# Second expert layer in pairs and single units of 128 slots, with results stored per token and summed at the end

## The chip, the cores and the metric

The kernel runs on one core of a Trainium2 chip, in float32 with float16 pairs (a high and a low part) for the second expert layer. The metric is the device time of one execution in microseconds, the median of the runs shown.

## The reference

The program is two transformer-like layers over x of 4 x 256 tokens (1024 in all) and 256 channels. Each layer is attention on a conditioned x, then a mixture of experts on a conditioned x, both added to x. The change lies in the last step, the experts of the second layer:

```python
gate_weights = softmax(x @ Wg + bg)                      # 8 experts
topv, topi = top_k(gate_weights, 2)
h  = gelu(x @ W1[n] + b1[n])                              # 256 -> 512
h  = gelu(h @ W2[n] + b2[n])                              # 512 -> 512
eo = h @ W3[n] + b3[n]                                    # 512 -> 256
out = sum over n of eo[n] * comb[:, n]                    # comb: topv at topi, else 0
x = x + out
```

## The kernel before

All stages before are left as they are: the conditioning, the first layer's attention, its experts in 47 tiles of 128 slots, the second layer's attention. While the second layer's attention runs, the expert weights are split into float16 pairs and stored in DRAM (`split1`, 2 MB for each expert), and the tokens are routed in three parts (the first four blocks of 128 tokens, then two, then two): `choose1`, `sum_tiles`, `combine`, `place_rows` on VectorE, `ranks1` and `turn_combination` on TensorE. A token's row (high and low parts of 256 channels, its eight combination weights, its number) is scattered by GpSimd to the DRAM array `slots` (L521), once for each of its two experts, each expert having a region of 1024 rows. 16 such indirect DMAs are issued.

Then come 15 tiles (TILES) of 256 slots (SLOTS), enough for any split of 2048 rows over 8 experts. VectorE works out a table (the expert and the first row of each tile), and SP reads it for the addresses of its loads. For tile j:

- SP loads the rows (`tile_rows`, four buffers; from tile 4 on after `added`, that is when the stores of tile j-4 have landed) and the 2 MB of weights with the biases (`tile_weights`, three buffers; when the third layer of tile j-3 is done). All loads have the line of the helper `load`, L323.
- TensorE turns the rows (`turn_tile`, L2247), then `first`, `second`, `third`: 24, 48 and 24 matmuls (three products for each pair of high and low parts; all in the helper at L1668), weights stationary and 256 slots moving in the first two, and slots stationary, 256 channels moving in the third. The order is written out: second(j), turn_tile(j+2), first(j+1), third(j).
- ScalarE copies the turned rows (`tile_out`, L836), applies Gelu for each of four chunks of a layer (`hidden`, L844), and scales the results by the combination weight (`rows_weighed`, L853, into two buffers).
- VectorE picks the weights (`pick`, L1645 and L1647) and splits the hidden values into high and low (`split_hidden`, L1652 and L1654).
- GpSimd adds the results to `out` by an indirect DMA with an addition at the destination (L532). Two tiles may hold the same token, so each tile's stores wait until the earlier tile's have landed.

`out` holds the base rows beforehand: x plus the biases b3 weighed by the combination (`base_rows`, `base_bias` on TensorE, banks 2 to 5; the copy at L831 on ScalarE), which SP stores as one DMA of 1 MB (L450) before the first accumulating store. Tile 0's turn on TensorE waits until all four parts of the base are copied.

## Time and profile before

| | us |
|---|---|
| median of 3 runs | 1161.17 |
| lowest, highest | 1158.29, 1168.63 |
| profiled execution: span, first to last instruction | 1139.7 |
| what lies around the span, against the median | 21.5 |

The page gives the span of one profiled execution and no other time for it; the median of the runs is 21.5 us longer. Of this span TensorE is busy 85%, VectorE 71%, ScalarE 51%, GpSimd 19%. PE is a TensorE matmul, PEld its load of stationary weights, DVE VectorE, ACT ScalarE, POOL GpSimd, SP SyncE, which issues the plain DMAs. The tiles of the second expert layer fill the time from about 944 us to the end.

### The profile page before, as it was taken

To read this page: it belongs to the slowest core of one execution; us is meant where nothing else is said; L and a number is where in the kernel's file an instruction comes from. 1 tells how busy PE (TensorE), PEld (TensorE's weight loads), DVE (VectorE), ACT (ScalarE), POOL (GpSimd) and SP (SyncE) were. 2 spreads that over 40 slices of the span, in tenths; PEclk is the share of its full clock that TensorE was granted. 3 is DMA by queue.
4 is the path that set the end of the run, shared out by engine and by line. 5 is a ranking of instruction groups with operands and counts; after the bars stand their busy time and mean duration, and the time that the engine had idled before them with its cause. 6 is when DMAs were issued, how large, how long until landed. Compare 5 with 4: busy or idle time off the path is not lost.

```text
span 1139.7 us, 18485 instructions
## 1 busy us (share of the span) xinstructions
PE 972.8 (85%) x6328; PEld 699.0 (61%) x6328; DVE 809.2 (71%) x2082; ACT 580.9 (51%) x1444; POOL 211.1 (19%) x175
## 2 busy tenths in 40 slices
PE   3898989997998799789987889689889976998995
PEld 2677767776777677553655566423333365987884
DVE  7689888888888879983487885766666763554542
ACT  2398439844884488441232332147566723544542
POOL 1101110111011101047233333100000050323223
PEclk9999999999999989989999999979999978999998
DMA  9999700000000000034588885325455547777762
GB/s 264 241 233 231 180 1 1 2 1 1 1 1 1 1 2 1 1 137 169 178 273 269 268 279 168 136 98 199 163 205 207 189 145 279 231 224 206 245 202 28
DMA packets 75966, 161.31 MB, mean 142 GB/s; under 512 B 10706, under 2 KB 57310, under 8 KB 71776
## 3 DMA queue, kind: packets, MB, share of 16 engines
q1 hardware_dynamic: 66992, 145.52, 41.9%
q0 software_dynamic: 8880, 14.60, 5.0%
q8 instruction: 51, 0.84, 0.3%
q14 instruction: 43, 0.35, 0.1%
HBM read 127.68 MB, written 62.62 MB: 167 GB/s over the span
## 4 chain that ended last, share of the span: by engine, by line
PE 46%; DVE 19%; DMA 17%; ACT 7%; issue 5%; POOL 3%; SPq 2%; POOLq 0%; ACTq 0%; DVEq 0%
PE ps L1668 43%; DMA out<-arena 8%; DMA arena<-in_w0all 4%; DMA made<-arena 3%; DVE arena L1449 2%; POOL out L532 2%; DVE arena L1108 2%; DVE arena L1125 1%; DMA arena<-slots 1%; ACT arena L632 1%; DVE arena L1117 1%; POOL slots L521 1%; ACT arena L617 1%; DVE arena L1141 1%; DVE arena L1079 1%
## 5 line engine op out<-in xcount | busy, mean ns | idle before, releaser
L1668 PE MATMUL ps<-arena 128*128 128x256 f16 (+14 forms) x4712 | 764.7, 338 | 57.0 <-DMA arena<-in_w0all 18.4
L1668 PEld LDWEIGHTS ps<-arena 128*128 128x128 f32 (+8 forms) x4712 | 529.0, 148 | 224.6 <-issue 94.8
L1652 DVE CAST arena<-arena 128x256 f16<-128x256 f32 x120 | 37.4, 311 | 96.4 <-ACT arena L844 96.4
L1449 DVE TENSOR_REDUCE arena<-ps 128x4 f16<-128x1024 f32 (+1 forms) x48 | 58.8, 1228 | 50.5 <-PE ps L1668 50.4
L844 ACT ACTIVATE arena<-ps,arena 128x256 f32<-128x256 f32 x120 | 55.6, 473 | 57.9 <-PE ps L1668 57.7
L1141 DVE SCALAR_TENSOR_TENSOR arena<-arena 128x128 f32<-128x128 f32 x240 | 84.0, 412 | 0.5
L469 POOL TENSOR_TENSOR den<-den,backd 128x512 f32<-128x512 f32 x8 | 10.5, 1307 | 393.4 <-DVE euv L946 393.4
L632 ACT ACTIVATE arena<-ident,arena 128x128 f32<-128x128 f32 x256 | 81.0, 391 | 0.0
L532 POOL DMA_INDIRECT out<-arena x30 | 47.5, 1584 | 146.6 <-DMA out<-arena 84.5
L501 POOL DMA_INDIRECT made<-arena x47 | 53.0, 1128 | 105.9 <-DVE arena L1362 105.4
L751 ACT ACTIVATE arena<-ps 128x1024 f32<-128x1024 f32 x48 | 49.2, 1024 | 43.4 <-PE ps L1668 43.4
L1108 DVE SCALAR_TENSOR_TENSOR arena<-arena,ps 128x128 f32<-128x128 f32 (+1 forms) x128 | 47.2, 410 | 26.9 <-PE ps L1668 20.4
L965 DVE RECIPROCAL den<-den 128x128 f32<-128x128 f32 x64 | 56.6, 923 | 0.4
L1654 DVE TENSOR_TENSOR arena<-arena 128x256 f16<-128x256 f32 x120 | 51.1, 426 | 4.1
L521 POOL DMA_INDIRECT slots<-side x16 | 15.6, 973 | 204.8 <-DVE side L1535 200.2
L617 ACT ACTIVATE arena<-arena 128x128 f32<-128x128 f32 (+1 forms) x128 | 50.3, 440 | 0.0
L719 ACT ACTIVATE arena<-ps 128x176 f32<-128x176 f32 x47 | 14.9, 318 | 65.4 <-PE ps L1668 65.4
L1668 PE MATMUL ps<-causal,identb 128*128 128x256 bf16 x160 | 36.4, 311 | 12.9 <-DVE arena L1449 10.1
L610 ACT ACTIVATE arena<-arena 128x128 f32<-128x128 f32 (+1 forms) x128 | 47.3, 441 | 0.0
L1125 DVE TENSOR_TENSOR arena<-ident,arena 128x512 f32<-128x512 f32 x64 | 46.2, 727 | 0.1
L1117 DVE CUSTOM_DVE_ANT_0 arena<-arena 128x128 f32<-128x128 f32 (+1 forms) x128 | 46.3, 399 | 0.0
L1479 DVE TENSOR_TENSOR arena<-arena 128x512 f16<-128x512 f32 x64 | 42.4, 684 | 4.9 <-ACT arena L791 4.9
(283 smaller groups left out, 1255.2 us busy)
## 6 DMA issues: line engine op xcount, KB each, us to landing
arena<-split SPq DMA_DIRECT2D x14, 2048.0 KB, 9.2
arena<-in_w0all SPq DMA_DIRECT2D x47, 608.0 KB, 5.1
slots<-in_blank SPq DMA_DIRECT2D x17, 1040.0 KB, 16.5
arena<-in_w1all SPq DMA_DIRECT2D x16, 1024.0 KB, 6.6
split<-arena SPq DMA_DIRECT2D x32, 512.0 KB, 3.8
slots<-in_blank SPq DMA_DIRECT2D x9, 1072.0 KB, 18.7
arena<-slots SPq DMA_DIRECT2D x47, 130.0 KB, 3.4
side<-made SPq DMA_DIRECT2D x8, 512.0 KB, 5.2
```

Of the source, the lines that this page charges most:

```text
L501: pool.indirect_dma_start(made0[:], bass.IndirectOffsetOnAxis(ap=ids, axis=0), y0[:, j % Y0N], None, bounds_check=K0 * NT - 1, oob_is_err= ...
L532: pool.indirect_dma_start(out[:], bass.IndirectOffsetOnAxis(ap=ids, axis=0), ytok[:, j % 2, half], None, compute_op=ALU.add).then_inc(adde ...
L617: ins = act.activation(prob[:, n % 3, cols], prob[:, n % 3, cols], ACT.Copy, scale=rinv[:, n % 2, tt:tt + 1])
L632: ins = act.activation(diag_post[:, n % 4, 2 * tt + i], ident[:], ACT.Copy, scale=mixw[:, tt, 3, i, n:n + 1])
L844: act.activation(hfull[:, m], ps[:, m, 0:SLOTS], ACT.Gelu, bias=bias[:, j % 3, 4 * layer + m:4 * layer + m + 1]).then_inc(l_read, 1)
L965: st(dve.reciprocal(part, part))
L1108: ins = dve.scalar_tensor_tensor(logit[:, s, tiles[tt]], rankq[:, 0, tiles[tt]], mixw[:, tt, 0, 2, n:n + 1], ps[:, s, tiles[tt]], ALU.mult ...
L1117: ins = dve.tensor_tensor_reduce(logit[:, s, tiles[tt]], logit[:, s, tiles[tt]], second[:, s, tiles[tt]], -1.0, 3.0e38, ALU.add, ALU.min, ...
L1125: dve.tensor_tensor(diag_pre[:, n % 4].rearrange("p (t i) j -> p t i j", t=TT), spread(spread(ident[:], 1, 2), 1, TT), spread(mixw[:, :, 1 ...
L1141: ins = dve.scalar_tensor_tensor(dst, prob[:, n % 3, tiles[tt]], w, dst, ALU.mult, ALU.add)
L1449: dve.tensor_reduce(out, ps[:, at:at + 2].rearrange("p j (r s) -> p j r s", r=nr), X, ALU.max, negate=True).then_inc(max1_done, 1)
L1668: return pe.matmul(o, l, r, start=start, stop=stop, skip_group_check=shared)
```

## The change

The tiles become 23 units of 128 slots, in 16 tiles: 7 pairs (256 slots) and 9 singles (128 slots), in the fixed order pair, single, pair, single, pair, single, single, and so on. Each tile still loads its expert's 2 MB once. The table gives each expert's pairs first and its left-over unit as a single. The first two layers move 128 columns for a single; the third has one half.

The eight combination weights in a row are replaced by five numbers (first weight, twice the token's number, difference of the second weight to the first, one, and the second expert). `pick` works out a slot's weight and its destination: 2 x token + choice. Results go by plain indirect stores, up to eight tiles deep in `ytok`, to a DRAM array `made1` with a row for each token and choice. At the end SP loads `made1` in four parts of 512 KB, VectorE adds the two choices and the base rows, and SP stores `out` in four parts of 256 KB. The base rows stay in SBUF, tokens laid out eight to a partition, so `base_rows` and `base_bias` take columns with a step of 8. The first base rows now wait for all of x, and all four `base_bias` for the last combination. The store of base rows to `out` and the wait for it are gone. The rows of tiles 0, 1 and 2 are requested before the rest of tile 0's weights and before tile 1's; the second layer's weights of tile 0 are requested with the first layer's.

```diff
 TILES0 = (NT * K0 + E0 * (P - 1)) // P
 W0WORDS = 2 * 2 * I0 + 2 * C
 SHUNITS = 2 * (-(-SH0 // P))
-TILES = (NT * 2 + E1 * (SLOTS - 1)) // SLOTS
-ROW = C + E1 + 4
+UNITS = (NT * 2 + E1 * (P - 1)) // P
+PAIRS = (UNITS - E1) // 2
+SINGLES = UNITS - 2 * PAIRS
+TILES = PAIRS + SINGLES
+SIZES = [2, 1] * 2 + [2, 1, 1] + [2, 1] * 2 + [2, 1, 1] + [2, 1]
+assert SIZES.count(2) == PAIRS and SIZES.count(1) == SINGLES
+UNIT0 = [sum(SIZES[:j]) for j in range(TILES + 1)]
+TABLE_AT = [SIZES[:j].count(2) if n == 2 else PAIRS + SIZES[:j].count(1) for j, n in enumerate(SIZES)]
+SLOTS = 2 * P
+MADE = Y0N
+ROW = C + 5
...
+        def stored1(j):
+
+            first_layer = (TILES0 + MADE - 1 - j % MADE) // MADE
+            return 16 * (first_layer + sum(SIZES[i] for i in range(j % MADE, j + 1, MADE)))
 
...
 
             def tile_rows(j):
-                row = sp.value_load(table[0:1, 16 + j:17 + j], min_val=0, max_val=E1 * REGION + 3 * SLOTS)
+                t, n = TABLE_AT[j], SIZES[j]
+                row = sp.value_load(table[0:1, 16 + t:17 + t], min_val=0, max_val=(E1 + 2) * REGION - SLOTS)
                 if j >= 4:
-                    sp.wait_ge(added, 32 * (j - 3))
-                load(rows_in[:, j % 4], slots[bass.ds(row, SLOTS)].rearrange("(a p) c -> p a c", p=P), x_in1[j % 4])
+                    sp.wait_ge(XT_pe, j - 3)
+                    sp.wait_ge(w_picked, j - 3)
+                load(rows_in[:, j % 4, 0:n], slots[bass.ds(row, n * P)].rearrange("(a p) c -> p a c", p=P), x_in1[j % 4])
...
             sp.wait_ge(scattered, 16 * 2 * TAU)
-            tile_rows(0)
-            tile_rows(1)
+            for j in range(3):
+                tile_rows(j)
             tile_weights(0, 1)
-            tile_weights(1)
-            sp.wait_ge(base_ready, 4)
-            sp.dma_start(out[0:NT].rearrange("(a p) c -> p a c", p=P), base).then_inc(base_out, 16)
             for j in range(1, TILES):
-                if j > 1:
-                    tile_weights(j)
-                if j + 1 < TILES:
-                    tile_rows(j + 1)
+                tile_weights(j)
+                if j + 2 < TILES:
+                    tile_rows(j + 2)
+            for n in range(MADE):
+                sp.wait_ge(made_out[n], stored1(TILES - MADE + n))
+            both = made1[0:2 * NT].rearrange("(p a k) c -> p a k c", a=TAU, k=2)
+            for q in range(TAU // 2):
+                load(planes[:, 2 * q:2 * q + 2], both[:, 2 * q:2 * q + 2], x_in1[q])
+            rows = out.rearrange("(p a) c -> p a c", a=TAU)
+            for q in range(TAU // 2):
+                sp.wait_ge(out_summed, q + 1)
+                sp.dma_start(rows[:, 2 * q:2 * q + 2], base[:, 2 * q:2 * q + 2]).then_inc(out_stored, 16)
+            sp.wait_ge(out_stored, 16 * (TAU // 2))
 
...
             for j in range(TILES):
-                pool.wait_ge(x_in1[j % 4], 16 * (j // 4 + 1))
-                if j:
-                    pool.wait_ge(added, 32 * j)
-                for half in range(2):
-                    pool.wait_ge(y1_read, 2 * j + half + 1)
-                    ids = rows_in[:, j % 4, half, C + E1:C + E1 + 1].bitcast(U32)
-                    pool.indirect_dma_start(out[:], bass.IndirectOffsetOnAxis(ap=ids, axis=0), ytok[:, j % 2, half], None,
-                                            compute_op=ALU.add).then_inc(added, 16)
-            pool.wait_ge(added, 32 * TILES)
+                pool.wait_ge(w_picked, j + 1)
+                for half in range(SIZES[j]):
+                    pool.wait_ge(y1_read, UNIT0[j] + half + 1)
+                    ids = idslot[:, 2 * (j % 4) + half:2 * (j % 4) + half + 1]
+                    pool.indirect_dma_start(made1[:], bass.IndirectOffsetOnAxis(ap=ids, axis=0), ytok[:, j % MADE, half], None,
+                                            bounds_check=2 * NT - 1, oob_is_err=False).then_inc(made_out[j % MADE], 16)
+            for n in range(MADE):
+                pool.wait_ge(made_out[n], stored1(TILES - MADE + n))
...
                 st.settle()
-                st.tell(dve.tensor_tensor(rows_out[:, part, C:C + E1], placed[:, 0, part], placed[:, 1, part], ALU.add),
+                st(dve.tensor_copy(rows_out[:, part, C], top1[:, part, 0]))
+                st(dve.tensor_tensor(rows_out[:, part, C + 2], top1[:, part, 1], top1[:, part, 0], ALU.subtract))
+                st(dve.tensor_copy(rows_out[:, part, C + 4], idf1[:, part, 1]))
+                st.tell(dve.tensor_tensor(comb1[:, part], placed[:, 0, part], placed[:, 1, part], ALU.add),
                         comb_ready, told)
...
             def pick(j):
+                n, t, rows = SIZES[j], TABLE_AT[j], rows_in[:, j % 4]
                 dve.wait_ge(x_in1[j % 4], 16 * (j // 4 + 1))
-                st(dve.tensor_tensor(picked, rows_in[:, j % 4, :, C:C + E1], spread(mine[:, j], 1, 2), ALU.mult))
-                st.settle()
-                st.tell(dve.tensor_reduce(wslot[:, j % 4], picked, X, ALU.add), w_picked, j + 1)
-
-            def split_hidden(dst, c):
+                if j >= 4:
+                    dve.wait_ge(y1_read, UNIT0[j - 3])
+                    dve.wait_ge(made_out[j % MADE], stored1(j - MADE))
+                st(dve.scalar_tensor_tensor(picked[:, 0:n], spread(rows[:, 0:n, C + 4], 2, 2), tile_e[:, t:t + 1],
+                                            rows[:, 0:n, C + 2:C + 4], ALU.is_equal, ALU.mult))
+                st.settle()
+                st(dve.tensor_tensor(wslot[:, j % 4, 0:n], picked[:, 0:n, 0], rows[:, 0:n, C], ALU.add))
+                st.tell(dve.tensor_tensor(idslot[:, 2 * (j % 4):2 * (j % 4) + n], picked[:, 0:n, 1], rows[:, 0:n, C + 1],
+                                          ALU.add), w_picked, j + 1)
...
             for j in range(TILES):
                 pick(j)
-                split_hidden(h2, 4 + 8 * j)
+                split_hidden(h2, j, 4 + 8 * j)
                 if j + 1 < TILES:
-                    split_hidden(h1, 8 + 8 * j)
+                    split_hidden(h1, j + 1, 8 + 8 * j)
+            for q in range(TAU // 2):
+                both, here = planes[:, 2 * q:2 * q + 2], base[:, 2 * q:2 * q + 2]
+                dve.wait_ge(x_in1[q], 16 * (TILES // 4 + 1))
+                st(dve.tensor_tensor(both[:, :, 0], both[:, :, 0], both[:, :, 1], ALU.add))
+                st.settle()
+                st.tell(dve.tensor_tensor(here, here, both[:, :, 0], ALU.add), out_summed, q + 1)
...
             def base_rows(q):
                 for half in range(2):
-                    tok = slice((2 * q + half) * P, (2 * q + half + 1) * P)
+                    tok = slice(2 * q + half, NT, TAU)
                     for k in range(CT):
...
             project_out(B - 1)
-            base_rows(0)
-            base_rows(1)
             ranks1(slice(HEAD, HEAD + TT), 2)
             route(wg1, E1, 5, range(HEAD + TT, TAU))
             turn_rows(3)
-            pe.wait_ge(combT_ready, 1)
-            base_bias(0)
-            base_bias(1)
+            pe.wait_ge(x_done, 2 * B)
+            base_rows(0)
+            base_rows(1)
             pe.wait_ge(low_ready, 3)
             base_rows(2)
             ranks1(slice(HEAD + TT, TAU), 3)
@@ -2231,8 +2286,8 @@
             pe.wait_ge(low_ready, 4)
             base_rows(3)
             pe.wait_ge(combT_ready, 2)
-            base_bias(2)
-            base_bias(3)
+            for q in range(TAU // 2):
+                base_bias(q)
 
...
             def layer(j, n, src, nk, c):
+                slots_in = slice(0, SIZES[j] * P)
                 for m in range(4):
                     if c + m >= 4:
                         pe.wait_ge(l_read, c + m - 3)
                     for k in range(nk):
                         for a, b in ((0, 0), (0, 1), (1, 0)):
-                            ins = mm(ps[:, m, 0:SLOTS], weights(j, a, n, k, slice(m * P, (m + 1) * P)), src[:, b, k],
+                            ins = mm(ps[:, m, slots_in], weights(j, a, n, k, slice(m * P, (m + 1) * P)), src[:, b, k, slots_in],
...
@@ -2280,12 +2336,13 @@
                 pe.wait_ge(h_split, 8 * j + 8)
                 if j == 0:
                     pe.wait_ge(w_in1[0], 32)
-                for half in range(2):
-                    if j:
-                        pe.wait_ge(y1_read, 2 * (j - 1) + half + 1)
+                for half in range(SIZES[j]):
+                    u = UNIT0[j] + half
+                    if u >= 2:
+                        pe.wait_ge(y1_read, u - 1)
                     for k in range(4):
                         for a, b in ((0, 0), (0, 1), (1, 0)):
-                            ins = mm(ps[:, 4 + half, 0:C], h2[:, b, k, half * P:(half + 1) * P],
+                            ins = mm(ps[:, 4 + u % 2, 0:C], h2[:, b, k, half * P:(half + 1) * P],
                                      weights(j, a, 2, k, slice(0, C)), k + a + b == 0, k == 3 and a == 1)
```

## Rows read from the trace of the kernel before

**Rows 1.** The page, TensorE's granted clock in 40 slices, in tenths of full speed.

```profile
PEclk9999999999999989989999999979999978999998
```

**Rows 2.** The chain that ended last, in order of time: start us, us, what.

```profile
979.76 1.56 POOL out L532
...
981.63 8.75 DMA out<-arena
```

**Rows 3.** Timeline of TensorE, tiles: start us, us, instructions [idle before <-releaser].

```profile
953.21 5.41 PE L1668 MATMUL ps<-arena 128*128 128x256 f16 x48 [1.80 <-DVE arena L1654]
...
962.13 0.62 PE L2247 MATMUL ps<-ident,arena 128*128 128x128 f16 x8 [3.50 <-DMA arena<-slots]
962.58 10.64 PE L1668 MATMUL ps<-arena 128*128 128x256 f16 x96
973.06 0.61 PE L2247 MATMUL ps<-ident,arena 128*128 128x128 f16 x8
...
1101.35 0.62 PE L2247 MATMUL ps<-ident,arena 128*128 128x128 f16 x8 [0.66 <-DMA arena<-slots]
...
1124.28 2.79 PE L1668 MATMUL ps<-arena 128*128 128x256 f16 x24 [1.35 <-DVE arena L1654]
```

**Rows 4.** Windows: busy us of each engine, TensorE's clock, DMA share, GB/s.

```profile
936.00:962.00 26.00, 14.15 (x94) 10.77 (x93) 5.74 (x18) 8.20 (x13) 0.47 (x1) 0.73 0.84 287
...
1038.00:1050.00 12.00, 11.42 (x109) 10.03 (x108) 6.03 (x19) 5.75 (x12) 3.29 (x2) 1.00 0.75 221
...
1110.00:1122.00 12.00, 12.00 (x112) 10.77 (x110) 6.92 (x20) 5.42 (x12) 6.31 (x4) 1.00 0.29 33
```

**Rows 5.** DMA issues: KB each, median us to landing; last, the one load at 956.44.

```profile
arena<-split SPq DMA_DIRECT2D x14, 2048.0 KB, 9.2
...
split<-arena SPq DMA_DIRECT2D x32, 512.0 KB, 3.8
...
made<-arena POOLq DMA_INDIRECT x47, 4.9
...
DMA to landing us min/median/max: 10.6/10.6/10.6
```

**Rows 6.** Groups by shape, TensorE's loads of weights: count, busy us, mean ns.

```profile
L1668 PEld LDWEIGHTS ps<-arena 128*128 128x128 f16 x1440 | 141.1, 98 | 20.4 <-DVE arena L1654 3.7
```

**Rows 7.** Timeline of SP's queue, start of the tiles and one later tile.

```profile
948.09 0.51 SPq L450 DMA_DIRECT2D out<-arena  x1
...
992.22 0.33 SPq L323 DMA_DIRECT2D arena<-split  x1
```

**Rows 8.** Groups by shape, VectorE, nearest to a single's split.

```profile
L1425 DVE CAST arena<-arena 128x128 f16<-128x128 f32 x4 | 0.9, 227 | 0.1
L1432 DVE TENSOR_TENSOR arena<-arena 128x128 f16<-128x128 f32 x4 | 1.2, 292 | 0.1
```

**Rows 9.** Timeline, the base rows and the start of tile 0.

```profile
934.77 3.77 PE L1668 MATMUL ps<-arena 8*128 8x256 f32 x8 [2.61 <-DVE arena L1539]
...
944.01 1.01 PE L2247 MATMUL ps<-ident,arena 128*128 128x128 f16 x8 [5.47 <-DMA arena<-slots]
...
947.04 4.38 PE L1668 MATMUL ps<-arena 128*128 128x256 f16 x24
```

**Rows 10.** Timeline, the end of the first layer's tiles, and the last tile.

```profile
701.64 0.98 POOL L501 DMA_INDIRECT made<-arena  x1 [1.18 <-DVE arena L1362]
703.89 10.24 SPq L323 DMA_DIRECT2D side<-made  x8
...
707.67 0.69 DVE L1381 TENSOR_TENSOR side<-side 128x512 f32<-128x512 f32 x1 [6.80 <-DMA side<-made]
709.10 0.69 DVE L1381 TENSOR_TENSOR side<-side 128x512 f32<-128x512 f32 x1 [0.73 <-DMA side<-made]
...
1125.89 0.47 ACT L853 ACTIVATE arena<-ps,arena 128x256 f32<-128x256 f32 x1 [2.44 <-PE ps L1668]
1127.15 1.55 POOL L532 DMA_INDIRECT out<-arena  x1 [5.27 <-ACT arena L853]
```

175 lines of the change are left out of this document (100 added, 75 removed).

## The prediction, on record before the result

> **What bounds the kernel now.** I read the page's first two parts: TensorE is busy 85%, its granted clock is full but for a few slices [rows 1]. That is an average; the change touches only the last fifth of the span, so I went on to the chain that ended last [rows 2]. From 979.76 us on it alternates between GpSimd's issue of an accumulating store (1.56 us) and its landing (8.75 us and more), and the next tile's first store waits for that landing: with two issues a tile this comes round every 11.4 us or later. This is one limit.
>
> The second limit is TensorE itself [rows 3]. One tile's turn starts at 962.13, the next at 973.06: a period of 10.93 us in which TensorE does not stop: 8 turns of 128 columns in 0.45 us (56 ns each, each with its own load of weights), then 96 matmuls of 256 columns from 962.58 to 973.06, 109.2 ns each. From 962.13 to 1101.35 there are 12 periods, 139.22 us; 12 x 10.93 is 131.16, so the chain of stores adds only 8.1 us, visible as waits for the rows of a later tile (0.66 us at 1101.35). The idle TensorE that the chain can be charged with is small, since both limits are about equal: removing the chain alone is worth little, and shortening TensorE alone would leave the chain.
>
> The third candidate is the DMA. In 1038 to 1050 it is 0.75 busy at 222 GB/s [rows 4]. In 1110 to 1122, where no more weights come, three accumulating stores (131 KB each) take 0.29 of 12 us, 1.16 us apiece. Taking two of them out of a tile's 9.0 us leaves 6.7 us for 2.37 MB, 354 GB/s; in 936 to 962, with few of them, it is 287 GB/s at 0.84, or 342 GB/s. A 2 MB load needs the engines 6.2 us then, but its landing takes 9.2 us in the median [rows 5].
>
> **The change part by part.** *Tiles.* Before: 15 tiles of 256 slots, 30 units of 128. After: 7 pairs and 9 singles, 23 units in 16 tiles. A pair costs the old 10.93 us. A single has 72 matmuls of 128 columns, 12 of 256 and 4 turns. The trace has no matmul of 128 columns on these weights; the nearest are the turns, f16, 128 x 128, with a load each: 56 ns. So 72 x 0.056 + 12 x 0.109 + 0.22 = 5.5 us. Stage: 7 x 10.93 + 9 x 5.5 = 126.3 against 15 x 10.93 = 163.95: **-37.6 us**. The upper end for the 128-column matmul is the mean duration of one load, 98 ns [rows 6]; I take 56 because the turns have a load of the same size each and still follow each other every 56 ns, so a load's duration overlaps its neighbours.
>
> The Trainium skill, TensorE: Matmul & The Clock Gate, Back-to-back issue gap, gives about 81 ns sustained for a stream of load and 128-column matmul, and its section LDWEIGHTS gives P/1.2, which for 128 columns is an estimate of 107 ns. By the first the 648 matmuls would cost 16 us more than by the row, by the second 33 us more. The turns' 56 ns in this trace disagree with both.
>
> *Waits that go.* With plain stores in eight buffers nobody waits for a landing: the 8.1 us above go. At the start, TensorE ends the second layer of tile 0 at about 958.6 and waits 3.5 us for tile 2's rows [rows 3], which lie behind the 1 MB store of the base rows in the queue [rows 7]; the store goes and the rows are asked for before the weights. The last tile's 1.35 us before its third layer goes with the old kernel too: **-12.9 us** together.
>
> *Waits that come.* (a) Weights. They have three buffers: the load of tile j leaves when the third layer of j-3 is done. SP needs some 0.9 us more, an estimate (it issues the biases, then the weights, 0.33 us of issue each [rows 7]), then 9.2 to land: 10.1. Where j-2 and j-1 are a pair and a single, TensorE has second 5.25 or 2.7, first 1.34 or 2.62, third 2.62 or 1.31, second 2.7 or 5.25, and turns, some 12.5 us: covered. Where both are singles (twice), it has 2.69 + 1.34 + 1.31 + 2.69 + 0.67 = 8.7: 1.4 us late, 2.8 in all. (b) Splitting. ScalarE's Gelu and VectorE's split stand between a layer's last group and the next layer. For 256 columns this takes 1.35 us (the wait at 1124.28 [rows 3]); the cover is the third layer of the tile before, 2.62 behind a pair but 1.31 behind a single. VectorE's 0.67 us a chunk keeps pace with 0.66 of TensorE for a pair; for a single, 0.23 + 0.29 [rows 8] beside matmuls of 0.34 a chunk lags slightly. I allow 2 us (0 to 6), and 1.3 at the last tile, where no first layer covers. Together **+6.1 us**, between 1.3 and 11. ScalarE takes 0.47 us a chunk of 256 [rows 10] and less for 128, eight and some copies in a single's 5.5 us: under the bound. GpSimd's issues, 23 of about 1.1 us, are hidden, as are the two or three small VectorE steps that choose weight and address of a row.
>
> *The head.* Three small VectorE steps are added to each of three parts of the routing; the last two lie ahead of a wait of VectorE for TensorE's ranks, of about the same length. On TensorE the base rows of tiles 0 to 3 move behind the turn of the last rows, in the place of four of the base's bias products (some 1.9 us, half of the eight at 934.77 [rows 9]): 16 matmuls of 128 float32 columns, an estimate of 1.8 to 3.7 us from those, by the clock. All four bias products now come after the last combination: eight took 3.8 us at 934.77, so 16 take 7.5, after a table of tiles that is some five VectorE steps (1 us) longer. Tile 0's turn waits for that: 936 + 7.5 and the copy give 944.5, against 943.98 before [rows 9]; GpSimd's 16 scatters, which end at their own pace, and the load of tile 0's rows give about the same. Behind them are the first three loads of rows and the first weights. A TensorE that has not stopped for 5 us may get its full clock back earlier than before, where the first layer took 4.38 us for 24 matmuls at half clock: -1.8. The base rows' strided weights may cost a little. **+0.5 us** (-2 to +4).
>
> *The tail.* Before: last matmul 1126.9 (1124.28 and 24 x 0.109), end 1139.7, 12.8 us. After: last matmul, copy 0.5, GpSimd 0.8 later (1126.36 to 1127.15 [rows 10]), store landed and seen 2.25 us after (701.64 to 703.89, the same drain in the first layer [rows 10]), or 4.9 where the DMA is busy [rows 5]. Then four loads of 512 KB: the first is usable 3.8 us after issue, the next 1.43 us later [rows 10], so the last at 8.1; two additions of 0.69; 0.5 to SP; a store of 256 KB, 3.4 us, from 512 KB at 3.8. Sum 0.5 + 0.8 + 2.25 + 8.1 + 1.5 + 0.5 + 3.4 = 17.05: **+4.3 us** (+2 to +8).
>
> Sum: -37.6 - 12.9 + 6.1 + 0.5 + 4.3 = -39.6 us. The profiled execution has a span of 1139.7; the median of the runs shown is 21.5 above it, which I leave as it is. 1161.2 - 39.6 = 1121.6, say **1121.5 us**, 3.4% faster.
>
> **Rivals.** *The load of weights sets the pace.* There are 16 loads of 2 MB instead of 15, in less time. If a load can't overlap the one before, 13 loads (tiles 3 to 15) at 9.2 us run from 10 us after the start of tile 0's second layer to 129.8; the last third layer is done 9 us later, 10 us after my 129 for this stretch. At the 10.6 us that a load took beside other traffic (the last of [rows 5]) it is 28 us. That gives 1131 to 1150. For it: 38 MB in 128 us is near 300 GB/s. Against: the 342 to 354 GB/s above, and the accumulating stores go, 35 us of engine time. *The narrow matmul is paced by its load*: 648 x (98 - 56) ns = 27 us, 1149. Against it are the turns' 56 ns. The Trainium skill's two figures above would put it at 1137 and 1155. *The clock falls.* The granted clock was 0.73 in 936 to 962, where TensorE was busy 14.15 of 26 us, and 1.00 through all of the later waits for rows [rows 4]. If waits for weights were dense enough to hold it at half (1.2 GHz), each microsecond of work costs another; the 39.6 us are gone once a third of the 123 us of work run at half, and with all of it the time is some 1240. That is the way to slower; nothing in the stretches at full clock supports it.
>
> **How the numbers follow.** Forecast 0.66, loads pace 0.19, narrow matmuls 0.09, clock 0.04, and 0.02 that the reordered head stalls more than I see (the change's stage then gives back less). The forecast's own bounds: added waits down to 1.3, head -2 and tail +2 give 1112; 11, +4 and +8 give 1134. The range reaches to 1110 for the scatter of the runs and to 1140 for half of the loads' rival, and leaves out the upper half of it and the 98 ns case. About 1% (1149.6 us and 1172.8 us) is what a measurement of this kernel can tell from no change, its runs lie 10 us apart. Faster by over 1%: 0.66 and most of 0.19 and of the 98 ns case: 0.91. Within 1%: 0.05; slower: 0.04.
>
> **What would show it.** The accumulating stores' waits are gone from the chain, TensorE dominates it up to the last 17 us. Matmuls of 128 columns start 56 ns apart; from tile 0's second layer to the last third layer 129 us. Weight waits appear before tiles 7 and 14, of 1 to 3 us; if they stand before every tile, it is the loads' rival, with the DMA share over 0.9. The granted clock is 1.00 throughout. Tile 0 is turned at 944 to 946. The prediction is wrong if singles take clearly more than 5.5 us, if 2 MB loads land in over 11 us while others are under way, or if the drain at the end is over 20 us.

## The result, and the profile after

The changed kernel takes 1128.38 us in the median of its runs (1115.46 to 1130.91), the kernel before 1161.17 us (1155.19 to 1168.63): a ratio of 0.970, 95% interval 0.965 to 0.976. That is 3.0% faster by the ratio, and 32.8 us less by the medians; 1121.5 us was forecast, with a range of 1110 to 1140. A ratio counts only executions within 1.5% of the fastest of their kernel; on chip A below, that leaves four of the thirteen of the kernel before, so the ratios there are cautious and their intervals wide.

The profiled execution has a span of 1113.6 us and took 1115.46 us, so only 1.9 us lie around the span. The profile of before has 1139.7 us, 21.5 below its median; if as little lies around that span, the gap is inside it. It was then an execution of some 1141.6 us, 13.6 below the fastest of its five runs. Its chip is not on record. So I compare stretches of the traces, not whole spans. Four stretches give the whole difference of the spans: up to the first turned combination 923.47 against 916.69 (+6.8, in code that the change hardly touches); from there to tile 0's second layer 41.87 against 36.52 (+5.3); from there to the last matmul 132.3 against 173.7 (-41.4); from there to the end 15.95 against 12.8 (+3.2). The sum is -26.1, as 1113.6 - 1139.7.

The windows of the changed kernel: the tiles, twelve microseconds out of them, and the end (busy us of PE, PEld, DVE, ACT, POOL, then the granted clock, DMA share, GB/s).

```profile
965.00:1098.00 133.00, 125.98 (x1484) 113.91 (x1484) 76.06 (x297) 65.04 (x161) 21.79 (x22) 1.00 0.69 249
1040.00:1052.00 12.00, 11.35 (x131) 10.24 (x129) 6.45 (x25) 5.68 (x13) 1.92 (x2) 1.00 0.67 256
1098.00:1113.00 15.00, 0.00 (x0) 0.00 (x0) 5.35 (x8) 0.42 (x1) 0.98 (x1) 0.58 0.59 210
```

TensorE works 95% of the tiles' stretch, at full clock throughout. The DMA is busy 0.69 of it, and in the twelve microseconds 0.67, less than the 0.75 of before [rows 4] with 35 GB/s more moved. The timeline of TensorE (start, us, instructions, [idle before <- what ended it]):

```profile
965.34 5.41 PE L1725 MATMUL ps<-arena 128*128 128x256 f16 x48 [1.35 <-DVE arena L1704]
970.59 0.61 PE L2302 MATMUL ps<-ident,arena 128*128 128x128 f16 x8
971.04 6.80 PE L1725 MATMUL ps<-arena 128*128 128x128 f16 x96
977.68 0.39 PE L2302 MATMUL ps<-ident,arena 128*128 128x128 f16 x4
977.90 4.09 PE L1725 MATMUL ps<-arena 128*128 128x256 f16 x36
982.56 5.41 PE L1725 MATMUL ps<-arena 128*128 128x256 f16 x48 [0.56 <-DVE arena L1704]
...
1016.60 2.85 PE L1725 MATMUL ps<-arena 128*128 128x128 f16 x48 [0.66 <-DVE arena L1704]
1019.29 0.39 PE L2302 MATMUL ps<-ident,arena 128*128 128x128 f16 x4
1019.51 9.63 PE L1725 MATMUL ps<-arena 128*128 128x256 f16 x84
...
1096.34 1.48 PE L1725 MATMUL ps<-arena 128*128 128x256 f16 x12 [1.83 <-DVE arena L1704]
```

Read the group of 96 at 971.04: tile 1's first layer (24 of 128 columns), tile 0's third (24 of 256), tile 1's second (48 of 128). It runs to the turn at 977.68, 6.64 us; with 24 x 0.1092 for the wide ones, a narrow one takes 56 ns. The only things that end an idle time of TensorE in this stretch are VectorE's splits (L1704), 7.6 us in ten rows with the 1.35 at its start. No row waits for weights: the first layer of tile 7 starts at 1019.51, right behind the turn.

The end, from all engines' timeline:

```profile
1099.25 0.98 POOL L555 DMA_INDIRECT made<-arena  x1 [5.03 <-ACT arena L880]
1101.45 1.76 SPq L340 DMA_DIRECT2D fac<-made  x4
1105.37 0.69 DVE L1716 TENSOR_TENSOR fac<-fac 128x512 f32<-128x512 f32 x1 [9.09 <-DMA fac<-made]
1106.82 4.50 SPq L481 DMA_DIRECT2D out<-arena  x4
1110.27 0.69 DVE L1718 TENSOR_TENSOR arena<-arena,fac 128x512 f32<-128x512 f32 x1
```

From the last matmul (1097.65) to the last store's issue 1.6 us, 2.2 until its landing is seen, 3.9 to the first addition, 5.6 over the four parts, 2.6 for the last store.

### The profile page after: what moved, and what is told of

Read it like the earlier page. It is cut to its first block, busy times and chain, and to the rows that moved or that the text cites. A ratio compares the mean times of both kernels' runs of the same rounds, so it can differ in the third digit from the quotient of the medians.

```text
span 1113.6 us, 18547 instructions
## 1 busy us (share of the span) xinstructions
PE 946.8 (85%) x6288; PEld 676.7 (61%) x6288; DVE 804.9 (72%) x2140; ACT 566.4 (51%) x1446; POOL 186.1 (17%) x168
## 4 chain that ended last, share of the span: by engine, by line
PE 54%; DVE 22%; DMA 9%; ACT 8%; issue 5%; SPq 1%; another core or an unknown queue 0%; POOL 0%; ACTq 0%; POOLq 0%; DVEq 0%
PE ps L1725 50%; DMA made<-arena 4%; DMA arena<-in_w0all 3%; DVE arena L1475 2%; DVE arena L1134 2%; DVE arena L1704 2%; DVE arena L1151 1%; ACT arena L656 1%; DVE arena L1143 1%; ACT arena L641 1%; DVE arena L1167 1%; DVE den L991 1%; DVE arena L1105 1%; ACT arena L634 1%; DVE arena L1702 1%
## 5 line engine op out<-in xcount | busy, mean ns | idle before, releaser
L1725 PE MATMUL ps<-arena 128*128 128x128 f32 (+15 forms) x4700 | 739.3, 333 | 64.6 <-DMA arena<-in_w0all 17.2
L1725 PEld LDWEIGHTS ps<-arena 128*128 128x128 f32 (+8 forms) x4700 | 505.6, 149 | 228.8 <-issue 99.6
L1702 DVE CAST arena<-arena 128x128 f16<-128x128 f32 (+1 forms) x128 | 32.8, 256 | 67.1 <-ACT arena L870 57.2
L870 ACT ACTIVATE arena<-ps,arena 128x128 f32<-128x128 f32 (+1 forms) x128 | 48.1, 418 | 49.1 <-PE ps L1725 44.4
L528 POOL DMA_INDIRECT made<-arena x47 | 53.0, 1127 | 107.8 <-DVE arena L1388 106.4
L1134 DVE SCALAR_TENSOR_TENSOR arena<-arena,ps 128x128 f32<-128x128 f32 (+1 forms) x128 | 47.2, 410 | 26.9 <-PE ps L1725 20.4
L548 POOL DMA_INDIRECT slots<-side x16 | 15.6, 972 | 208.2 <-DVE side L1564 203.9
L1704 DVE TENSOR_TENSOR arena<-arena 128x128 f16<-128x128 f32 (+1 forms) x128 | 45.3, 354 | 4.4
L1725 PE MATMUL ps<-causal,identb 128*128 128x256 bf16 x160 | 36.4, 311 | 12.8 <-DVE arena L1475 10.1
L1505 DVE TENSOR_TENSOR arena<-arena 128x512 f16<-128x512 f32 x64 | 42.5, 684 | 4.7 <-ACT arena L815 4.5
L555 POOL DMA_INDIRECT made<-arena x23 | 22.8, 990 | 130.8 <-DVE arena L1695 110.6
```

Of the source, the lines that this page charges most:

```text
L528: pool.indirect_dma_start(made0[:], bass.IndirectOffsetOnAxis(ap=ids, axis=0), y0[:, j % Y0N], None, bounds_check=K0 * NT - 1, oob_is_err= ...
L1134: ins = dve.scalar_tensor_tensor(logit[:, s, tiles[tt]], rankq[:, 0, tiles[tt]], mixw[:, tt, 0, 2, n:n + 1], ps[:, s, tiles[tt]], ALU.mult ...
L1704: st.tell(dve.tensor_tensor(dst[:, 1, m, 0:n], hfull[:, m, 0:n], dst[:, 0, m, 0:n], ALU.subtract), h_split, c + m + 1)
L1725: return pe.matmul(o, l, r, start=start, stop=stop, skip_group_check=shared)
```

## The experiments

Every ratio is to the kernel before, run on the same chip. The kernels ran in three groups, each on one chip: A (the first four below), B (the next four), C (the last four). The stretches are those of above, "head" from the first turned combination to tile 0's second layer, all in us.

| kernel | chip | median | ratio, interval | head | tiles | end |
|---|---|---|---|---|---|---|
| before, changed | - | 1161.2, 1128.4 | 0.970 (0.965 to 0.976) | 36.5, 41.9 | 173.7, 132.3 | 12.8, 15.9 |
| changed_again | A | 1125.8 | 0.974 (0.961 to 0.986) | 41.9 | 132.2 | 16.3 |
| pairs_only | A | 1157.3 | 1.001 (0.994 to 1.009) | 42.5 | 161.9 | 16.1 |
| rows_first | A | 1123.6 | 0.972 (0.963 to 0.982) | 39.1 | 132.4 | 15.9 |
| base_late | A | 1122.8 | 0.970 (0.955 to 0.984) | 42.2 | 132.4 | 15.8 |
| adding_chain | B | 1108.3 | 0.965 (0.962 to 0.969) | 40.1 | 130.3 | 16.7 |
| singles_last | B | 1109.8 | 0.966 (0.963 to 0.970) | 40.3 | 132.6 | 16.1 |
| pad_dve | B | 1105.8 | 0.964 (0.959 to 0.968) | 39.8 | 128.6 | 15.9 |
| rows_turns | B | 1104.5 | 0.962 (0.959 to 0.965) | 37.8 | 127.3 | 15.8 |
| changed_third | C | 1121.5 | 0.969 (0.962 to 0.975) | 41.9 | 132.2 | 16.0 |
| pairs_adding | C | 1158.0 | 0.995 (0.990 to 0.999) | 42.1 | 161.9 | 16.9 |
| rows_turns_again | C | 1126.1 | 0.969 (0.965 to 0.974) | 39.1 | 131.4 | 15.9 |
| three_edits | C | 1121.5 | 0.966 (0.960 to 0.971) | 38.7 | 131.5 | 15.9 |

The chip of the first row is not on record. The three medians of the changed kernel lie 0.6% apart, the executions of one kernel on one chip up to 2.3% (before, on A); head and tiles of the changed kernel's traces on A and C agree within 0.1 us, the end within 0.4. Where an edit is worth under 5 us, its verdict therefore rests on the stretches.

**changed_again** and **changed_third** are the changed kernel itself.

> The changed kernel once more, on the chip that also runs the three variants below, so that their traces have a neighbour. Expected: a time of 1115 to 1131 us; from the start of tile 0's second layer to the last third layer 132 us, as in its first trace. If the 6.8 us by which everything before the tiles was later in that trace belongs to the change, it is there again; if it is the scatter of single executions, it is another number.

> The changed kernel again, as the base for the other three kernels of this call. From the ratios to the kernel before that it had so far (0.970 and 0.974) it should come out 2.6 to 3.3% below it. If VectorE's hole of 3.3 us ahead of the last logits belongs to the program, it is here too; the four runs without it so far were all variants on another chip than the rest, so if it belongs to the chip, this run has it or not with all three others.

Both repeat the gain, with intervals clear of 1, and both have the hole of VectorE: an idle time of 3.3 us ahead of the last logits, for which the trace shows no releaser in the program (its rows stand at base_late).

**pairs_only.** All tiles are pairs again (15 of 256 slots), with everything else of the change kept.

```diff
-PAIRS = (UNITS - E1) // 2
-SINGLES = UNITS - 2 * PAIRS
+PAIRS = (NT * 2 + E1 * (2 * P - 1)) // (2 * P)
+SINGLES = 0
...
-SIZES = [2, 1] * 2 + [2, 1, 1] + [2, 1] * 2 + [2, 1, 1] + [2, 1]
+SIZES = [2] * PAIRS
```

> The new way of storing and summing, with the old tiles: 15 pairs, no singles. If the narrow tiles carry the gain (my account), this gives nearly all of it back: 15 tiles of 10.93 us, 161 us from tile 0's second layer to the last third layer against 132, and a time near 1157 us, 0 to 1% under the kernel before. If the chain of adding stores was what bound the old kernel, freeing it is most of the gain: about 1135 us.

The whole gain is gone, while the tiles still are 11.8 us shorter than before (161.9 against 173.7). So the narrow units are worth 161.9 - 132.2 = 29.7 us. Of the 11.8 us by which the tiles are shorter otherwise, 9.3 are paid out again at both ends: +6.0 and +3.3.

**adding_chain.** The units kept, the stores to `made1` made adding ones, each tile's only after the landing of the tile's before (`made1` is filled with zeros early on).

```diff
                 pool.wait_ge(w_picked, j + 1)
+                if j:
+                    pool.wait_ge(made_out[(j - 1) % MADE], stored1(j - 1))
...
-                                            bounds_check=2 * NT - 1, oob_is_err=False).then_inc(made_out[j % MADE], 16)
+                                            bounds_check=2 * NT - 1, oob_is_err=False,
+                                            compute_op=ALU.add).then_inc(made_out[j % MADE], 16)
```

> The units are kept (7 pairs, 9 singles), but the results go by stores that add at the destination, as before the change, each tile's only after the earlier tile's have landed. My reading of the profile of before: an issue takes about 1.56 us (the first of a pair is joined by the second) and a landing 8.75 us, so the chain comes round every 11.4 us for a pair and about 10 us for a single. 16 tiles then last 7 x 11.4 + 9 x 10 = 170 us against the 132 us of the changed kernel: about 1128 + 38 = 1165 us, the whole gain gone, with TensorE idle behind it through the eight buffers only at the end. Rival (an adding store lands faster when there is less to move, so TensorE stays the bound): the stage stays within 5 us of 132, 1128 to 1135 us.

My expectation fell, the rival holds: 0.965, tiles of 130.3. That is 1.7 us above the 128.6 of pad_dve, the changed kernel but for the pad, on the same chip, and it is no cost of the chain: tile 0's second layer, before the first store, takes that much longer. The granted clock was 0.50 in its first 3.4 us, and 1.00 throughout in pad_dve. The same 48 matmuls in adding_chain, then in pad_dve:

```profile
961.19 7.07 PE L1730 MATMUL ps<-arena 128*128 128x256 f16 x48 [2.03 <-DVE arena L1709]
```

```profile
959.15 5.41 PE L1729 MATMUL ps<-arena 128*128 128x256 f16 x48 [1.72 <-DVE arena L1708]
```

GpSimd's timeline of adding_chain:

```profile
972.78 1.61 POOL L559 DMA_INDIRECT made<-arena  x1 [30.22 <-DVE arena L1700]
974.69 1.58 POOL L559 DMA_INDIRECT made<-arena  x1 [0.30 <-issue]
983.63 1.56 POOL L559 DMA_INDIRECT made<-arena  x1 [7.35 <-DMA made<-arena]
990.40 1.55 POOL L559 DMA_INDIRECT made<-arena  x1 [5.22 <-ACT arena L885]
```

A pair's round, from its first issue to the next tile's, is 10.9 us here, but a single's only 6.8 and then ended by ScalarE, not by the landing. Over all tiles a single's round takes 5.2 to 7.4 us, and the landing ends about half of them: one adding store needs less time to land than two behind each other. I had taken "about 10 us" for a single from a pair's row and only dropped one issue.

**pairs_adding.** The edits of pairs_only and adding_chain together.

> Both parts undone in the tiles: 15 pairs and the adding stores with the wait for the earlier tile's, on top of the new end. Alone, pairs cost the whole gain (ratio 1.0013), and the adding chain with units cost nothing (0.9653). Theory: the chain of adding stores is as long as TensorE's work in either kernel, 11.2 to 11.4 us for a pair and 6 to 7 for a single, so it costs little beside a pair too: tiles of 162 us (as with plain stores) plus up to 8 us, ratio 1.00 to 1.01. Rival: the chain alone was worth the 10 us by which the old stage (173.7) exceeds the new one with pairs (161.9): ratio 1.010 to 1.015.

The tiles are 161.9 us with adding stores as with plain ones. So the plain stores are worth nothing in them, with wide tiles either. TensorE stands still for no landing in this kernel. The DMA queues of the kernel before (965 to 1125), then of this one (985 to 1140), each with 28 stores: packets, MB, share of 16 engines; the last figure of the x28 row is the median us to landing.

```profile
q0 software_dynamic: 4032, 3.67, 16.0%
...
out<-arena POOLq DMA_INDIRECT x28, 9.4
```

```profile
q0 software_dynamic: 4032, 2.11, 9.4%
```

28 stores of 131 KB are 3.67 MB; 2048 rows of 1 KB are 2.1 MB. With the check of bounds, which the change adds to the store, the rows of empty slots (3840 slots for 2048 rows) move nothing.

In the kernel before, nine stalls of TensorE at its turns are for rows, 10.2 us together. The first, 3.5 us [rows 3], is for tile 2's rows, which lay behind the 1 MB store of the base rows in the queue; that store is gone in this kernel too. The other eight are for rows of a tile j that were asked for only once tile j-4's stores had landed. Now the rows wait only until the buffer has been turned and picked from, empty rows move nothing, and results have eight buffers instead of two. These carry the other 8 us. Which of them carries how much was not tried.

**rows_first.** The rows of tiles 0 to 2 are asked for ahead of the 1 MB of tile 0's second layer's weights, as before the change. The first layer's weights stay ahead of the rows.

```diff
-                        load(wtile[:, 0, :, one:two], parts[:, :, one:two], ld["shared"])
                         return
+                    load(wtile[:, 0, :, one:two], parts[:, :, one:two], ld["shared"])
```

> The 1 MB of tile 0's second-layer weights is requested after the rows of tiles 0 to 2, as before the change. If the rows wait in the DMA behind these weights (6.7 us from request to landing in the changed kernel, 2.9 before), tile 0's turn comes 3 to 4 us earlier after the request; tile 0's second layer follows 2 to 4 us earlier unless its weights are then late. If the rows were slow for another reason, nothing moves. The time: 2 to 4 us less, less than the scatter, so the trace decides.

The stretch to tile 0's second layer is 2.7 us shorter than in the changed kernel beside it. The change had asked for the second layer's weights of tile 0 early, and its rows wait behind them in the queue: they landed 6.7 us after their request, against 2.9 before. Not all of that comes back, since another limit is close behind: tile 0's turn now waits 0.69 us for ScalarE's copy of the base rows.

**base_late.** The base rows of tiles 0 to 3 go behind the second turned combination.

```diff
-            pe.wait_ge(x_done, 2 * B)
-            base_rows(0)
-            base_rows(1)
             pe.wait_ge(low_ready, 3)
...
             turn_combination(1)
+            pe.wait_ge(x_done, 2 * B)
+            base_rows(0)
+            base_rows(1)
             pe.wait_ge(low_ready, 4)
```

> The base rows of tiles 0 to 3 are computed after the last ranks and the last combination's turn instead of ahead of them. If these 16 float32 matmuls at the half clock hold back the ranks and so the last four scatters (3 us in the changed kernel's trace), GpSimd's wait of 3.7 us before its last four scatters goes and they end some 3 us earlier; the base itself is complete no earlier and may then bound tile 0's turn. Rival: the ranks wait for VectorE anyway and nothing moves.

Nothing moved: TensorE then waited 5.5 us for VectorE, which makes the input of the ranks. The cause stands in the trace of the changed kernel, VectorE's timeline: it sits idle ahead of the last logits (L1511), although the routing products had ended about 931.7.

```profile
931.12 0.17 DVE L1564 CAST side<-side 128x4 uint32<-128x4 f32 x1
934.58 0.17 DVE L1511 TENSOR_TENSOR side<-ps,arena 128x16 f32<-128x16 f32 x1 [3.29 <-remote]
```

**pad_dve.** 64 writes to unused columns, before the first layer's tiles, move VectorE's stream of instructions.

```diff
+            for n in range(64):
+                st(dve.memset(small[:, 48 + n % 16:49 + n % 16], 0.0))
+                if n % 16 == 15:
+                    st.settle()
             middle(0)
```

> 64 one-column writes into unused columns are put into VectorE's instruction stream before the first layer's tiles; they cost under 5 us where they stand (64 x about 0.06 us, and VectorE is not the bound there), and nothing else is changed. In every trace of the changed kernel VectorE stands still for 3.3 us with no visible releaser before the last part of the logits (line 1511), and the kernel before has no such hole. If the hole comes from the position of the instruction in the stream (its index is 2046, 2 short of 8 x 256), the pad moves it away: the ranks, the last scatters and the turn of tile 0 come up to 3 us earlier counted from the first turned combination, total 1125 to 1129. If it comes from something that VectorE really waits for, the hole stays where it is and the total is 1128 to 1133.

The hole is gone, but in all four traces of chip B, the three without the pad too. The timeline of singles_last on B, the same two instructions and then TensorE:

```profile
926.67 0.17 DVE L1564 CAST side<-side 128x4 uint32<-128x4 f32 x1
...
927.28 0.17 DVE L1511 TENSOR_TENSOR side<-ps,arena 128x16 f32<-128x16 f32 x1 [0.44 <-PE ps L1725]
...
927.99 5.82 PE L1725 MATMUL ps<-ident,xT 128*128 128x128 f32 x24
...
933.64 0.73 PE L1725 MATMUL ps<-side,before_after 128*128 128x16 f32 x6
934.23 0.60 PE L2252 MATMUL ps<-ident,side 128*8 128x128 f32 x4
934.41 0.17 DVE L1555 TENSOR_TENSOR side<-ps,arena 128x16 f32<-128x16 f32 x1 [2.25 <-PE ps L1725]
```

So the pad tells nothing of its own, and the position in the stream is refuted as the sole reason: the same instructions have the hole on A and C and not on B. Nor does it always stand there: in pairs_adding, on C, VectorE waits only 0.45 us before the last logits, but 1.23, 1.16 and 1.46 us at later instructions. singles_last does show what stands behind the hole: the 24 float32 products of the base rows (5.82 us) hold the ranks, and VectorE waits 2.25 us for them, where it waited 1.05 in the kernel before.

**singles_last.** `SIZES` is seven pairs, then nine singles.

> Same work, other order: seven pairs, then nine singles in a row. It asks what the alternation of pair and single is worth. A single is 6.2 to 7 us of TensorE, and every one needs 2 MB. Theory (loads overlap, the DMA engines need about 6.5 us for 2 MB, a load lands some 9 to 10 us after its request, three buffers): a little below the DMA's capacity, waits for weights of 0 to 1.4 us a single, 0 to 12 us in all, plus 0.7 us for each single behind a single in place of one behind a pair: 1128 to 1142 us, with DMA shares near 0.95 in the singles. Rival (a load cannot overlap the one before, 9.2 us apiece): 8 x (9.2 - 6.5) = 22 us and more, 1150 us or over. If neither wait shows, 1125 to 1131.

The singles' windows and two of their rows on TensorE:

```profile
1040.00:1050.00 10.00, 9.37 (x139) 8.42 (x137) 6.78 (x32) 5.52 (x15) 1.74 (x2) 1.00 1.04 423
1050.00:1060.00 10.00, 8.80 (x139) 8.17 (x136) 6.78 (x29) 6.05 (x17) 1.21 (x2) 1.00 0.93 326
```

```profile
1041.77 2.85 PE L1725 MATMUL ps<-arena 128*128 128x128 f16 x48 [0.31 <-DVE arena L1704]
...
1047.98 2.85 PE L1725 MATMUL ps<-arena 128*128 128x128 f16 x48 [0.17 <-DVE arena L1704]
...
1052.09 2.83 PE L1725 MATMUL ps<-arena 128*128 128x128 f16 x36 [1.02 <-DMA arena<-split]
```

A single comes round in 6.0 to 7.1 us, with 2 MB each at a DMA share about 1. The loads overlap, and the waits for weights (1.02, 0.44, 1.13) sum to 2.6 us, the low end of the 0 to 12 expected. The tiles take 4.0 us more than in pad_dve, but 1.7 of that is the granted clock in tile 0's second layer (48 matmuls in 7.08 us), as in adding_chain. The rival, a load that can't overlap the one before, is refuted; so is a large worth of the alternating order.

**rows_turns**, run on two chips. rows_first, and where tile j is a single, the turn of tile j+2 behind the first layer of tile j+1 (on ScalarE its copy likewise).

```diff
-                if j + 2 < TILES:
+                if j + 2 < TILES and SIZES[j] == 2:
                     turn_tile(j + 2)
                 if j + 1 < TILES:
                     first(j + 1)
+                if j + 2 < TILES and SIZES[j] == 1:
+                    turn_tile(j + 2)
                 third(j)
```

> Two edits together: the rows of tiles 0 to 2 are requested before the first 1 MB of weights (measured alone: tile 0's second layer starts 2.7 us earlier), and where tile j is a single, the turn of tile j+2 is put behind the first layer of tile j+1 instead of ahead of it, so that it covers the split before the next second layer. In the changed kernel seven such places wait 0.56 to 0.67 us for VectorE; the turn is 0.22 to 0.45 us. Theory: each shrinks by that, at the cost of the same cover before the third layer of the single, which had 0.3 us to spare: between 0 and 3 us less. 1128 - 2.7 - 1.5 = 1124 us. Rival (ScalarE's copy of the turned rows now stands ahead of the scaling of results, or the split before the third layer becomes late): no gain from the second edit or up to 3 us of loss, 1125 to 1129.

> The two edits of before, rows first and the turn behind the first layer where the tile is a single, now beside the changed kernel on one chip. In its trace the split waits in the tiles fell (2.97 us of waits in all against 6 to 7 in the changed kernel's, but on another chip). Theory: 2.7 us from the rows and 1 to 4 us from the turns, 4 to 6.5 us less than the changed kernel beside it. Rival: the fewer split waits belong to the chip, and only the rows' 2.7 us are left.

The rows' edit repeats (head -2.8 us on C; -1.9 on B, against pad_dve). The turns shorten the tiles by 1.3 us on B (127.3 against 128.6 in pad_dve) and 0.8 on C (131.4 against 132.2): the low end of what I expected. The tiles, now reached earlier, wait for weights instead: 1.9 us in two rows on B, 0.5 in one on C. In the medians nothing of it shows: 0.969 on both sides on C, with the median of this kernel 4.6 us above that of the changed one. On C seven waits for splits are left in the tiles (4.4 us), on B one (1.05): the fewer waits belong to the chip, as the rival had it.

**three_edits** adds base_late to them.

> The same two edits, and the base rows of tiles 0 to 3 behind the ranks and the second turned combination. That edit alone moved nothing (base_late) where VectorE had its hole of 3.3 us. Where the hole is absent, the ranks' input is ready at 930.85 us (line 1527) and TensorE takes it at 933.64, after 24 float32 matmuls of the base rows that stand in front. Theory: without the hole, the last scatters, and with them tile 0, come 2 to 2.8 us earlier than in the kernel with two edits, if TensorE gets the base rows done in the wait for the scatters' landing, 5 us long; with the hole 0. Rival: the base rows then end behind the landing of tile 0's rows and hold the turn of tile 0: 0 to 3 us slower.

On C, with the hole, the head gets 0.4 us shorter: TensorE does the base rows in its wait for the scatters, up to the biases' products, and the turn waits 1.3 us for rows (0.7 for ScalarE's copy of the base without the edit). Three edits together make the smallest ratio on C (0.966 against 0.969), but the intervals overlap widely; in the stretches it is 4.0 us better than the changed kernel. The case that I meant, this kernel without the hole, was not measured, since this kernel ran on a chip with it.

## Why the prediction was right, and where it was not

**Sum.** By stretches I had forecast +0.5 for the head, -44.4 for the tiles (-37.6 - 12.9 + 6.1) and +4.3 for the end. The trace gives +5.3, -41.4 and +3.2. The differences, +4.8, +3.0 and -1.1, are 6.7 us; the median is 6.9 above the forecast. That the two agree so closely is luck: the three stretches leave out the 6.8 us ahead of the head, and the traces are single executions. Nor are the two traces alike. That of before has none of the pauses told of below, like those on chip B; the first of the changed kernel has them, like those on A and C. Like against like, with pad_dve, the stretches give +3.3, -45.1 and +3.1, together -38.7 us against the forecast -39.6, and each of the three within 3 us.

**Tiles, narrow units: right.** 56 ns for a 128-column matmul with a load of its own, taken from the turns, is what was measured. The load's 98 ns [rows 6] are how long one load lasts and not the pace, so that rival is out. Net of the waits that narrow units bring, I had them at 37.6 - 6.1 = 31.5 us; pairs_only gives 29.7. On chip B the padded kernel, otherwise the changed one, has tiles of 128.6 us where I forecast 129.

**Waits that go: right sum, and a wrong reason for most of it.** My 12.9 us were 8.1 for the landing of the accumulating stores, 3.5 for rows behind the store of the base, and 1.35 at the last tile. pairs_only, without narrow units, has tiles 11.8 us shorter than before, where the first two make 11.6. The last tile's wait did not go: 1.36 us there, and 1.83 in the changed kernel. For the 3.5 the reason fits: the store is gone, the rows are asked for earlier, and the wait is gone. The step "With plain stores in eight buffers nobody waits for a landing: the 8.1 us above go" named the wrong part. pairs_adding has the adding stores and GpSimd's wait for landings, and its tiles are as short. By elimination, what held TensorE was the rows of a later tile, asked for behind `added`, together with landings that were slow while empty rows moved too; no run undid one of these alone. The check of bounds on the new store stood in the diff, and I did not price it.

**Waits for weights: covered by another wait.** 2.8 us were forecast before tiles 7 and 14; none came in the first trace. The need was about right: the third layer of tile 4 ends at 1009.4, the load of tile 7 goes out at 1010.24, and the first layer of tile 7 starts 10.1 us after the former. But my 8.7 us for the work between was short of the split waits that stand in it (0.27 and 0.66 in the rows, and smaller gaps). The two terms are not additive. On B, where one of those waits is absent, 0.27 us for weights shows before tile 7.

**Splits: too small.** 2 + 1.3 us forecast, 6.2 measured behind the start (ten rows with 7.6 in all, less 1.35), plus smaller gaps. The 6.2 hold the last tile's 1.83, forecast at 1.3. Six of the waits stand before a second layer behind a single, 0.56 to 0.67 us each in the first trace, and are there on A and C too. The two before the second layer of a single stand in pad_dve on B as well (0.70 us each); the four before a pair's don't, and the last tile waits 1.05 there instead of 1.83. What B lacks comes with a pause of ScalarE in the second layer of the single in front. The changed kernel, then the padded one on B:

```profile
975.87 0.37 ACT L870 ACTIVATE arena<-ps,arena 128x128 f32<-128x128 f32 x1 [0.20 <-PE ps L1725]
...
976.58 1.11 POOL L555 DMA_INDIRECT made<-arena  x1 [0.30 <-issue]
977.41 0.37 ACT L870 ACTIVATE arena<-ps,arena 128x128 f32<-128x128 f32 x1 [1.17 <-PE ps L1725]
```

```profile
969.68 0.37 ACT L870 ACTIVATE arena<-ps,arena 128x128 f32<-128x128 f32 x1 [0.19 <-PE ps L1729]
...
970.35 0.37 ACT L870 ACTIVATE arena<-ps,arena 128x128 f32<-128x128 f32 x1 [0.30 <-PE ps L1729]
970.38 1.11 POOL L555 DMA_INDIRECT made<-arena  x1 [0.30 <-issue]
```

Two chunks of Gelu start 0.67 us apart on B and 1.54 on the other chip, and TensorE goes on alike at this place: from the first of these two to the next turn it is 1.81 us in both. The pause stands beside GpSimd's second issue in these rows. So it does in all seven tiles with a second issue, with ScalarE idle for 1.1 to 1.9 us; in pad_dve, on B, in none of the seven. That the issue causes it was not tried. The tiles are 3.7 us longer with the pauses than in pad_dve.

**Head: +5.3, not +0.5.** This step failed, beyond its bound of +4; on B, without the holes, the head is +3.3 to +3.8, just inside it. The premise that failed is "GpSimd's 16 scatters, which end at their own pace". Before, they did. In the changed kernel GpSimd waits for the last ranks before its last four scatters. The last scatter in the kernel before, then the first of the last four in the changed one:

```profile
935.51 0.96 POOL L521 DMA_INDIRECT slots<-side  x1 [0.30 <-issue]
```

```profile
941.91 0.96 POOL L548 DMA_INDIRECT slots<-side  x1 [3.73 <-DVE side L1564]
```

The wait is 3.5 to 3.8 us in all traces of A and C, and 2.0 on B. Counted from the first turned combination the last scatter ends 3.4 us later than before (pad_dve: 1.7), from there to tile 0's turn it takes 1.9 us more (2.0), and from the turn to the second layer as long as before, 9.2 us (8.8 on pad_dve). These are the 5.3 us.

Behind them stand three things. The rows of tile 0 lie behind 1 MB of weights in the queue: 2.7 us by rows_first. The base rows lie ahead of the ranks: VectorE waits 2.25 us for the ranks on B and 1.05 before, where I had counted the products' own 1.8 to 3.7 us but not who waits behind them. And the hole, which covers that wait on A and C and adds to it: the head is 41.9 there and 39.8 to 40.3 on B, 1.6 to 2.1 us. The parts overlap, so they are not to be added up. The 1.8 us that I credited for an earlier full clock did not come either: the first layer's 24 matmuls took 5.27 us at a granted clock of 0.52 in the first trace, against 4.38 at 0.63 before.

**End: +3.2 for +4.3.** The sum's form was right. From the last addition to the end it took 2.6 us, where I had 0.5 for SP and 3.4 for the store; the rest came out 0.2 longer.

**The time itself.** The 21.5 us between span and median, "which I leave as it is", took scatter for a constant. It did no harm, because the difference was taken from the median in the end. Had I forecast the span of the next profile, I would have been wrong by it.

The rivals on the loads and the clock are out: no wait for weights in the changed kernel's traces and 0.27 us in pad_dve, and a granted clock of 1.00 in all of the changed kernel's tiles.

## What to carry to other kernels

Cutting padded work to half tiles pays in full only if the narrow instruction's interval really halves; an existing stream of the same shape in the trace (here the turns) says so beforehand. When two limits are equally long, look at each stall for the buffer or request that it waits for, and undo the parts one at a time: here the adding store looked like the limit, and undoing it alone cost nothing. Ask also who waits behind work that is moved: the base rows' products hold the ranks, and with them the last scatters. A transfer that is moved ahead is paid by the one that now stands behind it in the queue. Before you compare two traces, look whether code that the change leaves alone runs alike in both.

## What the runs showed of the hardware that I had not expected

The same instructions run with holes on some chips and without on another, also in code that no kernel here changes. The first layer's shared experts in 522 to 553 us, windows of rows_turns on B and of rows_turns_again, the same kernel, on C:

```profile
522.00:553.00 31.00, 29.60 (x92) 15.13 (x90) 8.66 (x14) 4.67 (x9) 18.42 (x19) 1.00 0.30 102
```

```profile
522.00:553.00 31.00, 17.75 (x42) 6.52 (x40) 7.32 (x13) 3.46 (x6) 18.71 (x20) 0.86 0.30 104
```

TensorE runs 92 matmuls in the one and 42 in the other; GpSimd does nearly the same in both (19 and 20 instructions). The timeline of the second, ScalarE between rows of GpSimd:

```profile
531.60 0.96 POOL L523 DMA_INDIRECT slots<-arena  x1 [0.30 <-issue]
532.45 0.60 ACT L720 ACTIVATE arena<-ps 128x512 f32<-128x512 f32 x1 [5.95 <-remote]
...
545.54 0.96 POOL L523 DMA_INDIRECT slots<-arena  x1 [0.30 <-issue]
548.64 0.60 ACT L720 ACTIVATE arena<-ps 128x512 f32<-128x512 f32 x1 [15.59 <-remote]
```

ScalarE's usual idle time before this copy is 2.84 us, on B each time. All traces of A and C and the first of the changed kernel have longer ones here, up to 15.6 us, those of B and of before none; in this stretch the first changed trace has 26.9 us of TensorE's work, before 29.5. The kernel before runs at 1148 us on B and at 1160 to 1164 on A and C, and on one chip its runs lie up to 27 us apart. The three kinds of hole that I found (here, VectorE's at the last logits, ScalarE's in the singles) have one thing in common: GpSimd is issuing indirect DMAs back to back, or issues a second one right behind the first. On B it does the same and these pauses are absent, so this can't be the whole cause. No run spaced these issues out; the cause stays open. The Trainium skill, Runtime: NRT & Kernel Launch, Instruction fetch mechanics, holds the fetch of instructions to be hidden where the code runs straight on. No run here ties the holes to the fetch or clears it.

The changed kernel's narrow matmuls bear on a figure: the Trainium skill, TensorE: Matmul & The Clock Gate, Back-to-back issue gap, gives about 81 ns for a stream of load and 128-column matmul. The stream here, 648 float16 matmuls of 128 columns, each with a load, takes 56 ns apiece in the group read above; the measurement decides.

An adding store of 128 rows costs GpSimd 1.55 us of issue, a plain one 0.98 us, and with plain stores the eight result buffers never ran out: no row of the changed kernel waits for a landing before the end.
